# A transformer block on one core: row statistics and normalisation moved ahead of the second tile's maximum in VectorE's order, and the first transposes of the probabilities waiting tile by tile

## The chip, the cores and the metric

The kernel runs on one core of a Trainium2 chip. The metric is the device time of one execution in microseconds, as the median over runs. TensorE (PE), VectorE (DVE), ScalarE (ACT) and GpSimd (POOL) each run their own list of instructions in order and wait for each other by semaphores; SyncE's queue (SP) issues nearly all transfers of the attention loop.

## The reference

One cross-attention block with a feed-forward part, in float32. x is 2 x 2048 x 512, the context 2 x 77 x 512, and there are 16 heads of 32.

```python
xq = layer_norm(x, qn_w, qn_b)
ctx = layer_norm(context, cn_w, cn_b)
q = (xq @ q_w).reshape(B, N, H, D)
kv = (ctx @ kv_w).reshape(B, M, 2, H, D)
attn = jnp.einsum('bnhd,bmhd->bhnm', q, k) * scale
attn = jnp.where(xa_mask[:, None, :, :], neg, attn)
attn = jax.nn.softmax(attn, axis=-1)
out = jnp.einsum('bhnm,bmhd->bnhd', attn, v).reshape(B, N, C)
x = x + out @ proj_w + proj_b
h = layer_norm(x, n2_w, n2_b)
h = gelu(h @ fc1_w + fc1_b) @ fc2_w + fc2_b
return x + h
```

## The kernel before

Every matrix product is made from three passes: each operand is split into a high part (rounded by ScalarE, names that end in h) and a low part (the rest, by VectorE, names that end in l).

The kernel has two stages. The first, the attention pipeline, works on 16 units of 256 rows (two tiles of 128). The second, the feed-forward part, works on 8 blocks of 512 rows and is not touched.

One step k of the pipeline works on four units at once. Of unit k it does the back part: transposes of the probabilities (`prob_T`, out of S), their split into PT (`prob_hi` on ScalarE, `prob_lo` on VectorE), the product with the values (`av`), the projection (`proj`) and the residual, which VectorE adds into xr. Of unit k+1 it does the scores (`score`, four head groups of each of two tiles), the masked copy into S (`masked`), the row maximum (`maximum`, on VectorE), the exponentials (`exps` for tile 0 and `exp_all` for tile 1 on ScalarE) and their normalisation by GpSimd. Of unit k+2 it does the transposes of the normalised rows (`x_T`), their split (`x_hi`, `x_lo`) and the query product (`q`). Of unit k+3 it does the layer norm: `stats` and `variance` on VectorE, `rstd` (a power) on GpSimd, and `normed`, which writes xhat, on VectorE.

Each engine's order is written out by hand in the function `step` of its program. Steps 0 to 9 run in a hardware loop of two steps a round; steps 10 to 15 are written out. Steps 10 to 13 also make one tile of the second layer norm for the feed-forward part (`norm2`: `h_stats`, `h_variance`, `h_normed`, `h_T`, `h_lo`), and steps 10 to 12 are the last with a layer norm of unit k+3. Two preparing steps (`prep`) come ahead.

The places that matter here:

- TensorE begins a step with a score group of tile 0, `x_T(0)`, a score group, `x_T(1)`, then `prob_T1(0, 0)` (three transposes), a score group, `prob_T1(0, 1)`, the last score group of tile 0, and `q(0)`. GpSimd's multiplication of S by 1/sum, one for each tile (L531), counts `p_prob`, and the first transpose waits for both.
- The transposes of the probabilities alternate between two PSUM banks: `v_probT.wait(pe, b, i - 2)`. So the two of group 3, `prob_T(3)`, wait until `prob_lo(2)` has read the banks of group 2, tile by tile. Likewise a score group waits for the masked copy two groups back.
- VectorE's `prob_lo(2)` (L858) stands behind `maximum(1)` (L835) and `av_lo(0)` (L863).
- GpSimd's step is: add the projection's bias to xr, write the mask as numbers, subtract tile 1's maximum from S (L517), `rstd` (L480), and the two multiplications (L531).
- SP stores unit k's result out of its slot of xr once the residual is done, waits for the store to land, and then loads unit k+4 into the same slot. `stats` of step k+1 works on unit k+4 and waits for this load:

```python
v_res.wait(sp, k, UT - 1)
sp.dma_start(x2_units[k.u]..., xr[...]).then_inc(d_x2st, 16)
if more:
    sp.wait_ge(d_x2st, k.q * 32 + (k.u * 16 + 16))
    load_x(k.plus(4))
...
def stats():
    dve.wait_ge(d_x[n.u], n.q * 16 + 16)      # n = k + 3
```

Of the kernel before, what the change touches and what calls it, by code (L numbers as in the profile page):

```python
# [26 lines left out]
P = 128  # L27
# [39 lines left out]
def build_block(nc, x, ctx, mask, qn_w, qn_b, cn_w, cn_b, n2_w, n2_b, q_w, kv_w, proj_w, proj_b,  # L67
# [10 lines left out]
    UT = 2  # L78
# [62 lines left out]
    veps = at("veps", [P, UT], F32)  # L141
    rstd = at("rstd", [P, UT], F32)
# [90 lines left out]
    p_prob = count("p_prob", UT)  # L233
# [15 lines left out]
    v_bn, v_mv, v_veps = count("v_bn", UT), count("v_mv", UT), count("v_veps", 1)  # L249
    p_rstd = count("p_rstd", 1)  # L250
    v_xhat = count("v_xhat", UT)
# [31 lines left out]
    def static(n):  # L283
        return Unit(n // 2, n % 2)
# [185 lines left out]
    def gpsimd_program(pool):  # L470
        pool.memset(mhalf[:, :], -0.5).then_inc(p_half, 1)
        pool.memset(ident[:, :], 0.0).then_inc(p_ident, 1)
        pool.wait_ge(p_ident, 1)
        pool.affine_select(out=ident[:, :], in_=ident[:, :], compare_op=ALU.not_equal, fill=1.0, base=0,
                           pattern=[[-1, P]], channel_multiplier=1).then_inc(p_ident, 1)
        pool.wait_ge(p_half, 1)

        def power(dst, src, n):

            return pool.tensor_tensor(dst, src, mhalf[0:n, 0:src.shape[1]], ALU.pow)  # L480

        pool.wait_ge(v_cve, 1)
        power(crs[0:M, :], cve[0:M, :], M).then_inc(p_crs, 1)
        for b in range(B):
            pool.memset(f32(vbd[:, b, :, :, :]).rearrange("p a b c -> p (a b c)"), 0.0).then_inc(p_zero, 1)

        def may_negate(n):

            pool.wait_ge(d_mask[n.u], n.q * 16 + 16)
            v_scores.wait(pool, n.plus(-2), UT * KT - 1)  # L490

        def negative(n):

            pool.tensor_scalar(negm[:, n.u, :, :], mask_in[:, n.u, :, :], -FLT_MAX, 1.0, ALU.mult,
                               ALU.mult).then_inc(p_neg.sem, 1)

        def step(k, back=False, scores=False, front=False, norm=False, prep=None,
                 norm2=None, split=()):
            def add_projb(t):
                v = xr[:, bass.ds(k.slot(), 1), t, :]  # L500
                pool.tensor_tensor(v, v, projb[:, :].unsqueeze(1), ALU.add).then_inc(p_projb.sem, 1)

            if front:
                may_negate(k.plus(2))
            if back:
                add_projb(0)
            if front:
                negative(k.plus(2))
            if back:
                add_projb(1)  # L510
            if norm2 is not None:
                h_rstd(static(0), norm2)
            if scores:
                n = k.plus(1)
                v_max.wait(pool, n, 1)
                v = S[:, n.u, 1, :].rearrange("p (h m) -> p h m", h=H)
                pool.tensor_tensor(v, v, nmax[:, n.u, 1, :].unsqueeze(2).to_broadcast([P, H, M]),  # L517
                                   ALU.add).then_inc(p_less.sem, 1)
            if norm2 is not None:
                h_bias(static(0), norm2)  # L520
            if norm:
                n = k.plus(3)
                v_veps.wait(pool, n, 0)
                v_xhat.wait(pool, n.plus(-1), UT - 1)
                power(rstd[:, :], veps[:, :], P).then_inc(p_rstd.sem, 1)
            if scores:
                n = k.plus(1)
                for t in range(UT):
                    v_rsum.wait(pool, n, t)
                    v = S[:, n.u, t, :].rearrange("p (h m) -> p h m", h=H)  # L530
                    pool.tensor_tensor(v, v, rsum[:, n.u, t, :].unsqueeze(2).to_broadcast([P, H, M]),  # L531
                                       ALU.mult).then_inc(p_prob.sem, 1)
            if prep == "scores":
                pool.wait_ge(d_projb, 16)

        def h_rstd(n, t):
            v_hve.wait(pool, n, t)
            power(hrs[:, :], hve[:, :], P).then_inc(p_hrs.sem, 1)

        def h_bias(n, t):  # L540

            if isinstance(n.q, int) and n.q == 0 and n.u == 0 and t == 0:
                pool.wait_ge(d_fc2b, 16)
            v_hhat.wait(pool, n, t)
            v = x2[n.u][:, t, :]
            pool.tensor_tensor(v, v, fc2b[:, :], ALU.add).then_inc(p_fc2b.sem, 1)

        pipeline(pool, step)


        def step2(s, first=False, last=False):
            for j in range(JT):
                if not last and j in NORMS:
                    h_rstd(s.plus(1), NORMS.index(j))
                    h_bias(s.plus(1), NORMS.index(j))

        blocks(pool, step2)
# [193 lines left out]
    def vector_program(dve):  # L751
# [10 lines left out]
        for b in range(B):  # L762
            i = dve.bn_stats(cbn[0:M, b, :], cx[0:M, b, :])
        i.then_inc(s_chain, 1)
        dve.wait_ge(s_chain, 1)
        for b in range(B):
            i = dve.bn_aggr(cmv[0:M, b, :], cbn[0:M, b, :])
# [4 lines left out]
        for b in range(B):  # L772
            i = dve.tensor_scalar(cx[0:M, b, :], cx[0:M, b, :], cmv[0:M, b, 0:1], crs[0:M, b:b + 1],  # L773
                                  ALU.subtract, ALU.mult)
# [43 lines left out]
        def step(k, back=False, scores=False, front=False, norm=False, prep=None,  # L818
                 norm2=None, split=()):
            b, s, f, n = k, k.plus(1), k.plus(2), k.plus(3)  # L820

            def masked(t, g_):
                i = t * KT + g_
                if i == 0:
                    p_neg.wait(dve, s, 0)
                    t_probT.wait(dve, s.plus(-2), KT * UT - 1)
                t_scores.wait(dve, s, i)
                dve.tensor_tensor(S[:, s.u, t, g_ * GM:(g_ + 1) * GM].rearrange("p (h m) -> p h m", h=HG),  # L828
                                  s_bank(i, prep)[:, 0:GM].rearrange("p (h m) -> p h m", h=HG),
                                  negm[:, s.u, t, :].unsqueeze(1).to_broadcast([P, HG, M]),  # L830
                                  ALU.add).then_inc(v_scores.sem, 1)
# [20 lines left out]
            def prob_lo(g_, tiles=range(UT)):  # L852
                for t in tiles:
                    i = g_ * UT + t
                    v = slice(t * P, (t + 1) * P)
                    a_probT.wait(dve, b, i)
                    slots, n = new_slots(g_)
                    dve.tensor_tensor(PT[LO][:, slots, v], bT[i % 2][:, 0:n * P].rearrange("p (c n) -> p c n", c=n),  # L858
                                      f32(PT[HI][:, slots, v]), ALU.subtract).then_inc(v_probT.sem, 1)
# [18 lines left out]
            def stats():  # L878
                dve.wait_ge(d_x[n.u], n.q * 16 + 16)
                for t in range(UT):  # L880
                    dve.bn_stats(bnst[:, t, :], xr[:, bass.ds(n.slot(), 1), t, :]).then_inc(v_bn.sem, 1)

            def variance():
                for t in range(UT):
                    dve.bn_aggr(mv[:, t, :], bnst[:, t, :]).then_inc(v_mv.sem, 1)
                v_mv.wait(dve, n, UT - 1)
                dve.tensor_scalar(veps[:, :], mv[:, :, 1], EPS, None, ALU.add).then_inc(v_veps.sem, 1)
# [44 lines left out]
                h_variance(static(0), norm2)  # L932
            if back:
                prob_lo(0, (1,))
            if scores:
                masked(1, 0)
                masked(1, 1)
            if back:
                prob_lo(1)
            if scores:  # L940
                masked(1, 2)
                masked(1, 3)
            if prep == "scores":
                maximum(0)
                x_lo(0)
                x_lo(1)
# [19 lines left out]
                prob_lo(3)  # L966
            if norm2 is not None:
                h_normed(static(0), norm2)
            if norm and prep is None:
                stats()  # L970
                v_bn.wait(dve, n, UT - 1)
            if back:
                av_lo(2)
            if split:
                w1_lo(split[1])
            if norm and prep is None:
                variance()
            if front:
                q_lo(1)
            if back:  # L980
                av_lo(3)
            if scores and prep is None:
                recip(0)
            if norm and prep != "q":
                normed()
            if prep == "scores":
                values_lo(1)
            if scores and prep is None:
                exp_sum()
# [84 lines left out]
    def tensor_program(pe):  # L1074
# [40 lines left out]
        def step(k, back=False, scores=False, front=False, norm=False, prep=None,  # L1115
# [33 lines left out]

            def prob_T1(g_, t):  # L1150
                i = g_ * UT + t
                if i == 0:
                    p_prob.wait(pe, b, UT - 1)
                v_probT.wait(pe, b, i - 2)
                for n, c in enumerate(NEW[g_ % 2]):
                    r = g_ // 2 * 2 * GM + START[c]
                    mm = pe.transpose(bT[i % 2][:, n * P:(n + 1) * P], S[:, b.u, t, r:r + P], ident[:, :])  # L1157
                mm.then_inc(t_probT.sem, 1)
# [194 lines left out]
```

## Time and profile before

| | |
|---|---|
| median of 3 runs | 1138.02 us (1137.82 to 1138.62) |
| span of the profiled execution | 1135.9 us |
| TensorE busy | 1100.3 us (97%) |
| VectorE busy | 606.5 us (53%) |
| ScalarE busy | 404.4 us (36%) |
| GpSimd busy | 234.7 us (21%) |
| mean granted TensorE clock | 0.997 |

The profile is of one execution, whose own time is its span of 1135.9 us; around it lie some 2 us that the runs' times hold besides. Busy shares are means over the two stages. VectorE's busy share by fortieths of the span is 7 to 9 tenths over the attention pipeline (the first 15 slices) and 2 to 4 tenths behind it.

### The profile page before, as it was taken

Reading aid. Unit: us, or ns where it says so; the run is one execution under the profiler, and the core shown is the slowest. Engines: PE = TensorE matmul, PEld = TensorE weight load, DVE = VectorE, ACT = ScalarE, POOL = GpSimd, SP = SyncE. Lnnn points to the kernel's source line nnn. Section 1 sums busy time; section 2 is a strip of 40 time slices with the busy share of each in tenths; the row PEclk is TensorE's granted clock in tenths of the full one; section 3 lists DMA queues with packets and bytes.
Section 4 is the critical chain, followed back from the end, with each engine's and each line's share of the span. In section 5 each row is a group of like instructions: output and inputs, shape, how many; then the busy total and the mean of one; then the engine's idle time right before and its main releaser. Section 6 shows DMA issues by size and latency. Waiting matters only on the chain.

```text
span 1135.9 us, 16366 instructions
## 1 busy us (share of the span) xinstructions
PE 1100.3 (97%) x5849; PEld 941.0 (83%) x5849; DVE 606.5 (53%) x1154; ACT 404.4 (36%) x1158; POOL 234.7 (21%) x186
## 2 busy tenths in 40 slices
PE   4999999999999999999999999999999999999998
PEld 4789988999889888888888888888888888888887
DVE  7898999899999765632423322323333333232212
ACT  3456655566666744421211311221221131121110
POOL 2343444444554420100100100100110110010000
PEclk9999999999999999999999999999999999999999
DMA  7011111232111024202002002002001001100101
GB/s 245 8 35 58 38 38 47 65 93 65 39 57 39 29 91 145 71 19 74 1 1 75 1 2 74 1 1 74 1 1 64 13 1 38 38 1 1 38 1 38
DMA packets 40144, 48.76 MB, mean 43 GB/s; under 512 B 10965, under 2 KB 19197, under 8 KB 40087
## 3 DMA queue, kind: packets, MB, share of 16 engines
q1 hardware_dynamic: 37919, 43.74, 11.7%
q10 hardware_dynamic: 2168, 4.21, 1.0%
q8 instruction: 42, 0.69, 0.2%
q14 instruction: 15, 0.12, 0.0%
HBM read 30.54 MB, written 16.78 MB: 42 GB/s over the span
## 4 chain that ended last, share of the span: by engine, by line
PE 85%; DVE 5%; POOL 4%; issue 3%; ACT 2%; DMA 0%; ACTq 0%; POOLq 0%; DVEq 0%
PE bank L1304 31%; PE bank L1275 31%; PE bank L1144 7%; PE bank L1175 6%; POOL S L531 4%; PE bank L1125 4%; PE bank L1157 3%; ACT S L637 1%; PE bank L1186 1%; PE bank L1287 1%; DVE xhat L893 1%; DVE cx L773 1%; DVE esum L868 0%; PE bank L1135 0%; DVE S L828 0%
## 5 line engine op out<-in xcount | busy, mean ns | idle before, releaser
L1304 PE MATMUL bank<-w,gTh 128*128 128x512 f32 x1024 | 319.3, 393 | 0.0
L1045 DVE CAST gTh<-g 128x512 fp32r<-128x512 f32 x128 | 56.9, 444 | 442.9 <-ACT g L739 442.9
L739 ACT ACTIVATE g<-bank,cols 128x512 f32<-128x512 f32 x128 | 88.0, 688 | 471.6 <-PE bank L1275 470.1
L1304 PEld LDWEIGHTS bank<-w,gTh 128*128 128x128 f32 x1024 | 192.4, 188 | 42.7
L1304 PE MATMUL bank<-w,gTl 128*128 128x512 f32 x512 | 200.4, 391 | 0.0
L1275 PE MATMUL bank<-hT0h,w 128*128 128x512 f32 x512 | 162.2, 397 | 0.0
L1275 PE MATMUL bank<-hT1h,w 128*128 128x512 f32 x512 | 159.1, 392 | 0.1
L480 POOL TENSOR_TENSOR hrs<-hve,mhalf 128x1 f32<-128x1 f32 x32 | 17.6, 549 | 551.3 <-DVE hve L1019 551.3
L1304 PEld LDWEIGHTS bank<-w,gTl 128*128 128x128 f32 x512 | 96.1, 188 | 22.0
L1275 PEld LDWEIGHTS bank<-hT0h,w 128*128 128x128 f32 x512 | 94.7, 188 | 21.5
L1275 PEld LDWEIGHTS bank<-hT1h,w 128*128 128x128 f32 x512 | 95.1, 188 | 19.8 <-issue 0.5
L637 ACT ACTIVATE S<-S,nmax 128x77 f32<-128x77 f32 x256 | 88.9, 354 | 41.8 <-DVE nmax L835 41.8
L1275 PE MATMUL bank<-hT0l,w 128*128 128x512 f32 x256 | 101.1, 395 | 0.0
L1275 PE MATMUL bank<-hT1l,w 128*128 128x512 f32 x256 | 99.7, 389 | 0.0
L1053 DVE TENSOR_TENSOR gTl<-g,gTh 128x512 fp32r<-128x512 f32 x128 | 88.6, 693 | 4.5
L531 POOL TENSOR_TENSOR S<-S,rsum 128x1232 f32<-128x1232 f32 x32 | 75.1, 2346 | 46.1 <-DVE rsum L876 46.1
L1144 PE MATMUL bank<-xTh,wqh 128*128 128x256 f32 x256 | 74.7, 292 | 0.1
L1175 PE MATMUL bank<-PTh,vbd 128*128 128x256 f32 x384 | 73.3, 287 | 0.6 <-DVE PTl L858 0.6
L1144 PE MATMUL bank<-xTl,wqh 128*128 128x256 f32 x256 | 72.8, 285 | 0.0
L1144 PE MATMUL bank<-xTh,wql 128*128 128x256 f32 x256 | 72.8, 284 | 0.0
L723 ACT ACTIVATE bank<-bank,cols 128x128 f32<-128x128 f32 x128 | 47.2, 428 | 66.8 <-PE bank L1287 66.8
L858 DVE TENSOR_TENSOR PTl<-bank,PTh 128x256 fp32r<-128x256 f32 (+1 forms) x128 | 57.6, 482 | 12.0 <-ACT PTh L622 12.0
(103 smaller groups left out, 1824.8 us busy)
## 6 DMA issues: line engine op xcount, KB each, us to landing
xr<-in_x SPq DMA_DIRECT2D x16, 512.0 KB, 3.5
x_scratch<-xr SPq DMA_DIRECT2D x16, 512.0 KB, 2.8
x<-x_scratch SPq DMA_DIRECT2D x8, 1024.0 KB, 5.6
out<-x SPq DMA_DIRECT2D x7, 1024.0 KB, 4.3
w1raw<-in_L_xattn_fc_w SPq DMA_DIRECT2D x16, 256.0 KB, 3.0
w2raw<-in_L_xattn_fc_w SPq DMA_DIRECT2D x16, 256.0 KB, 2.6
kvw<-in_L_xattn_kv_w ACTq DMA_DIRECT2D x2, 1024.0 KB, 11.1
qraw<-in_L_xattn_q_w ACTq DMA_DIRECT2D x1, 1024.0 KB, 11.6
```

The costliest lines, as they stand in the source:

```text
L531: pool.tensor_tensor(v, v, rsum[:, n.u, t, :].unsqueeze(2).to_broadcast([P, H, M]), ALU.mult).then_inc(p_prob.sem, 1)
L637: i = act.activation(v, v, ACT.Exp, bias=nmax[:, s.u, t, h:h + 1], accum_out=esum[:, s.u, t, h:h + 1])
L723: i = act.activation(v, v, ACT.Identity, bias=cols[:, N2B + k:N2B + k + 1], scale=cols[:, N2W + k:N2W + k + 1])
L739: act.activation(g[:, :], bF[j % 2][:, :], ACT.Gelu, bias=cols[:, F1B + j:F1B + j + 1]).then_inc(a_gelu.sem, 1)
L858: dve.tensor_tensor(PT[LO][:, slots, v], bT[i % 2][:, 0:n * P].rearrange("p (c n) -> p c n", c=n), f32(PT[HI][:, slots, v]), ALU.subtract) ...
L1045: dve.tensor_copy(gT[HI][j % 4][:, :], g[:, :]).then_inc(v_ghi.sem, 1)
L1053: dve.tensor_tensor(gT[LO][j % 4][:, :], g[:, :], f32(gT[HI][j % 4][:, :]), ALU.subtract).then_inc(v_glo.sem, 1)
L1125: mm = pe.matmul(s_bank(i, prep)[:, 0:GM], qT[d][:, g_, t * P:(t + 1) * P], kbd[w][:, s.u, g_, :], start=(n == 0), stop=(n == 2))
L1144: mm = pe.matmul(bA[m // 2][:, (m % 2) * UN:(m % 2 + 1) * UN], wq[w][:, c, m * P:(m + 1) * P], xT[d][:, c, :], start=(n == 0), stop=(n == ...
L1175: mm = pe.matmul(bV[g_ % 2][:, 0:UN], vbd[:, b.u, w, g_ * NC + c, :], PT[d][:, slot(g_, i), :], start=(n == 0), stop=(n == 3 * NC - 1))
L1275: mm = pe.matmul(bF[j % 2][:, :], w1[:, j, w, c, :], hT[s.u][d][:, c, :], start=(c == 0 and i == 0), stop=(c == KT - 1 and i == 2))
L1304: mm = pe.matmul(bC[t][:, :], gT[d][j % 4][:, t * P:(t + 1) * P], w2[:, j, w, :], start=(j == 0 and i == 0), stop=(j == JT - 1 and i == 2))
```

## The change

In VectorE's order of the steps with a layer norm (all but the preparing ones), `stats` moves from behind the split of group 3 of the probabilities to ahead of the masked copies of tile 1, `variance` to behind the first two of these, and `normed` to ahead of `maximum(1)`. It used to stand behind the reciprocal of tile 0's sums, ahead of tile 1's sums. GpSimd's `rstd` moves ahead of the subtraction that waits for `maximum(1)`. On TensorE the transposes of group 0 wait for the probabilities of their own tile alone.

```diff
 GpSimd
             if norm2 is not None:
                 h_rstd(static(0), norm2)
+            if norm and prep is None:
+                x_rstd()
             if scores:
                 n = k.plus(1)
                 v_max.wait(pool, n, 1)
...
-            if norm:
-                n = k.plus(3)
-                v_veps.wait(pool, n, 0)
-                v_xhat.wait(pool, n.plus(-1), UT - 1)
-                power(rstd[:, :], veps[:, :], P).then_inc(p_rstd.sem, 1)
+            if norm and prep is not None:
+                x_rstd()
 VectorE
             if back:
                 prob_lo(0, (1,))
+            if norm and prep is None:
+                stats()
             if scores:
                 masked(1, 0)
+            if norm and prep is None:
+                v_bn.wait(dve, n, UT - 1)
+            if scores:
                 masked(1, 1)
+            if norm and prep is None:
+                variance()
             if back:
                 prob_lo(1)
             if scores:
                 masked(1, 2)
                 masked(1, 3)
+            if norm and prep is None:
+                normed()
...
             if norm2 is not None:
                 h_normed(static(0), norm2)
-            if norm and prep is None:
-                stats()
-                v_bn.wait(dve, n, UT - 1)
             if back:
                 av_lo(2)
             if split:
                 w1_lo(split[1])
-            if norm and prep is None:
-                variance()
...
-            if norm and prep != "q":
+            if prep == "scores":
                 normed()
-            if prep == "scores":
                 values_lo(1)
 TensorE
             def prob_T1(g_, t):
                 i = g_ * UT + t
-                if i == 0:
-                    p_prob.wait(pe, b, UT - 1)
+                if g_ == 0:
+                    p_prob.wait(pe, b, t)
                 v_probT.wait(pe, b, i - 2)
```

VectorE, the middle of a loop step, from the second split of group 0 (`prob_lo(0, (1,))`) to the split of group 2. `S` is the masked copy, `nmax` the maximum, `PTl` the low part of the transposed probabilities, `aTl` that of the product with the values. Before:

```order
L858 TENSOR_TENSOR PTl<-bank,PTh 128x3x128 [waits a_probT]
...
L828 TENSOR_TENSOR S<-bank,negm 128x308 [waits t_scores] x2
...
L858 TENSOR_TENSOR PTl<-bank,PTh 128x2x128 [waits a_probT]
...
L828 TENSOR_TENSOR S<-bank,negm 128x308 [waits t_scores]
...
L835 TENSOR_REDUCE nmax<-S 128x16 [waits v_scores]
L64 ISA
L863 TENSOR_TENSOR aTl<-bank,aTh 128x256 [waits a_av]
```

The same place of VectorE now (the lines have moved by 5). `bnst`, `mv` and `veps` are the row statistics, `xhat` the normalised rows:

```order
L863 TENSOR_TENSOR PTl<-bank,PTh 128x3x128 [waits a_probT]
L884 ISA
L886 ISA [waits d_x1]
L886 BN_STATS bnst<-xr 128x6
...
L833 TENSOR_TENSOR S<-bank,negm 128x308 [waits t_scores,v_bn]
L890 BN_AGGR mv<-bnst 128x2 x2
L892 TENSOR_SCALAR veps<-mv 128x2 [waits v_mv]
...
L898 TENSOR_SCALAR xhat<-xr,mv,rstd 128x512 [waits t_xT,p_rstd]
L898 TENSOR_SCALAR xhat<-xr,mv,rstd 128x512 [waits t_xT]
L64 REGISTER_ALU
L840 TENSOR_REDUCE nmax<-S 128x16 [waits v_scores]
```

Seven instructions and the wait for the load of x (`d_x1`, in the other step of a round `d_x0`) now stand between the split of group 0 and that of group 2, which comes right behind the rows shown.

GpSimd, the middle of a loop step, before (`nmax` is the subtraction of the maximum, `rstd` the power):

```order
L501 TENSOR_TENSOR xr<-xr,projb 128x512
L64 ISA
L517 TENSOR_TENSOR S<-S,nmax 128x1232 [waits v_max]
L64 ISA
L64 ISA [waits v_veps]
L480 TENSOR_TENSOR rstd<-veps,mhalf 128x2 [waits v_xhat]
```

and now:

```order
L501 TENSOR_TENSOR xr<-xr,projb 128x512
L64 ISA
L64 ISA [waits v_veps]
L480 TENSOR_TENSOR rstd<-veps,mhalf 128x2 [waits v_xhat]
L64 ISA
L525 TENSOR_TENSOR S<-S,nmax 128x1232 [waits v_max]
```

The power no longer stands behind the wait for the maximum.

## Rows read from the trace of the kernel before

**Rows 1.** Page, busy time of each engine and share of the span
```profile
PE 1100.3 (97%) x5849; PEld 941.0 (83%) x5849; DVE 606.5 (53%) x1154; ACT 404.4 (36%) x1158; POOL 234.7 (21%) x186
```

**Rows 2.** Timeline of TensorE, around a step's start: start, duration, [idle before <-releaser]
```profile
208.95 0.60 PE L1157 MATMUL bank<-ident,S 128*128 128x128 f32 x4
209.31 0.48 PE L1175 MATMUL bank<-PTh,vbd 128*128 128x256 f32 x2
...
218.23 0.39 PE L1186 MATMUL bank<-wph,aTl 128*128 128x512 f32 x1
...
219.73 0.60 PE L1135 MATMUL bank<-ident,xhat 128*128 128x128 f32 x4
221.43 0.55 PE L1157 MATMUL bank<-ident,S 128*128 128x128 f32 x3 [1.09 <-POOL S L531]
...
227.07 0.39 PE L1125 MATMUL bank<-kbdh,qTh 128*128 128x308 f32 x1
...
291.34 0.55 PE L1157 MATMUL bank<-ident,S 128*128 128x128 f32 x3 [1.08 <-POOL S L531]
```

**Rows 3.** Timeline of GpSimd, the two multiplications of S of that step
```profile
214.62 2.51 POOL L531 TENSOR_TENSOR S<-S,rsum 128x1232 f32<-128x1232 f32 x1 [0.99 <-DVE rsum L876]
219.12 2.25 POOL L531 TENSOR_TENSOR S<-S,rsum 128x1232 f32<-128x1232 f32 x1 [2.00 <-DVE rsum L876]
```

**Rows 4.** Timeline of VectorE, layer norm at the end of the step
```profile
210.57 1.27 DVE L881 BATCH_NORM_STATS2 bnst<-xr 128x6 f32 x2
...
212.31 0.24 DVE L885 BATCH_NORM_AGGREGATE mv<-bnst 128x2 f32<-128x6 f32 x2
212.58 0.17 DVE L887 TENSOR_SCALAR veps<-mv 128x2 f32<-128x2 f32 x1
...
214.47 2.94 DVE L893 TENSOR_SCALAR xhat<-xr,mv,rstd 128x512 f32 x2
```

**Rows 5.** Timeline of VectorE, preparing step: the same pair with GpSimd idle
```profile
31.73 1.00 DVE L893 TENSOR_SCALAR xhat<-xr,mv,rstd 128x512 f32<-128x512 f32 x2
```

**Rows 6.** Timeline of VectorE, residual and first half of the next step
```profile
219.16 1.29 DVE L901 TENSOR_TENSOR xr<-bank,xr 128x512 f32 x2
...
221.13 1.28 DVE L841 TENSOR_TENSOR xTl<-bank,xTh 128x512 fp32r<-128x512 f32 x2
...
223.60 0.55 DVE L858 TENSOR_TENSOR PTl<-bank,PTh 128x384 fp32r<-128x384 f32 x1
...
225.40 0.55 DVE L858 TENSOR_TENSOR PTl<-bank,PTh 128x384 fp32r<-128x384 f32 x1
225.87 0.85 DVE L828 TENSOR_TENSOR S<-bank,negm 128x308 f32<-128x308 f32 x2
227.55 0.76 DVE L858 TENSOR_TENSOR PTl<-bank,PTh 128x256 fp32r<-128x256 f32 x2 [0.83 <-ACT PTh L622]
...
229.11 1.44 DVE L835 TENSOR_REDUCE nmax<-S 128x16 f32<-128x1232 f32 x1
...
230.80 1.01 DVE L858 TENSOR_TENSOR PTl<-bank,PTh 128x384 fp32r<-128x384 f32 x2
```

**Rows 7.** Timeline of ScalarE, the high part of `x_T(1)`
```profile
220.37 0.60 ACT L603 ACTIVATE xTh<-bank 128x512 fp32r<-128x512 f32 x1 [0.27 <-PE bank L1135]
```

**Rows 8.** Timeline of SP's queue, the store of x2 and the load of x
```profile
220.75 0.39 SPq L408 DMA_DIRECT2D x_scratch<-xr  x1
223.89 0.38 SPq L369 DMA_DIRECT2D xr<-in_x  x1
```

**Rows 9.** Instructions of line L369, the load of x: issue to landing
```profile
DMA to landing us min/median/max: 3.1/3.5/9.5
```

**Rows 10.** Timeline of TensorE, starts of steps 11 and 12
```profile
313.44 0.63 PE L1135 MATMUL bank<-ident,xhat 128*128 128x128 f32 x4 [0.74 <-DVE hT0l L1030]
...
337.12 0.63 PE L1135 MATMUL bank<-ident,xhat 128*128 128x128 f32 x4 [0.74 <-DVE hT0l L1030]
```

More of the change, by code:

```diff
@@ L510, in step, with x_rstd @@
                 add_projb(1)
+            def x_rstd():
+                n = k.plus(3)
+                v_veps.wait(pool, n, 0)
+                v_xhat.wait(pool, n.plus(-1), UT - 1)
+                power(rstd[:, :], veps[:, :], P).then_inc(p_rstd.sem, 1)
             if norm2 is not None:
                 h_rstd(static(0), norm2)
+            if norm and prep is None:
+                x_rstd()
             if scores:
```

## The prediction

> **What bounds the kernel now.** I read the page first: TensorE is busy for 1100 of 1136 us [rows 1], so only what makes it wait, or takes a wait away, can move the time. The change touches the 16 steps of the attention pipeline alone, about the first 400 us. Next the timeline of TensorE, for what stands in front of its waits. A loop step holds one: after `x_T(1)` it waits for the first transpose of the probabilities, and the profile puts the wait on GpSimd's multiplication of S [rows 2]. The transposes of `x_T(1)` start at 219.73; with no wait the next group follows 0.36 us behind (the step 208.95 to 209.31, also four transposes), at 220.08, but it starts at 221.43: 1.35 us lost. From 221.43 to 291.34 are three steps [rows 2], so a step takes 23.30 us.
>
> Then I ask why the multiplication is late. GpSimd had nothing to do for 2.00 us before tile 1's [rows 3]: it waited for VectorE's sums, which stand behind `normed`. And `normed`, two instructions, took 2.94 us [rows 4], while the same pair takes 1.00 us where GpSimd is idle [rows 5]: in the loop it coincides with the multiplication of tile 0 [rows 3], and its second instruction gets through only when that is done.
>
> **The change, part by part.** I count in us behind the start of `x_T(1)` on TensorE (219.73 in the rows; "at 5.0" is 224.73). The sum is made against the profiled execution (span 1135.9, and 2.1 us more in the median of the runs, 1138.0).
>
> Removed. The tile 1 sums no longer wait for `normed`, so they come up to 2.9 us earlier and the wait of 1.35 us at `prob_T1(0, 0)` goes; I give it back whole. The wait by tiles then costs and brings nothing more: both multiplications are done when TensorE arrives. Without any wait a step would be 21.95 us, and TensorE would reach the score group of tile 1 that stood at 227.07 at 5.99, and `prob_T(3)` at 11.17 (the step's 23.30, less 10.78 from 208.95 to 219.73, less 1.35) [rows 2].
>
> Moved. `stats`, `variance` and `normed` now stand ahead of `prob_lo(2)`, for which `prob_T(3)` waits. So the question is when VectorE has done `prob_lo(2)`. I follow it through the step:
>
> - ScalarE's high part of `x_T(1)` ends at 1.24 [rows 7]; the low part takes 0.64 (half of 1.28), to 1.9; two masked copies 0.8 (0.85 less their overlap with the next), to 2.7; the first split of group 0, the maximum of tile 0 and the second split 0.46 + 1.36 + 0.46 (from 225.40 to 225.87, and 229.11 to 230.80 less the 0.33 of the split between), to 5.0 [rows 6].
> - Now `stats`. It reads x of unit k+3, whose load SP issues only after the residual of the step before is stored. The residual ended at 220.45, and the load was issued at 223.89, 3.44 us later [rows 6, 8]; it lands 3.1 to 3.5 us after that [rows 9], so at 7.3 to 7.7 by the old timing. The old `stats` began at 210.57, some 14 us into the step, and never saw this [rows 4]. In the new order the second residual is no longer held by VectorE but by the projection, whose last matmul ends at 218.62 [rows 2]; with 0.05 for the semaphore and 0.65 for the instruction (half of 1.29) [rows 6] it ends at -0.4, and x lands at 6.1 to 6.5. I take 6.2, a little below the middle, as a choice. VectorE waits 1.2 us, and everything behind it on its queue with it: the masked copies that free the score banks, the splits, the maximum.
> - From 6.2: `stats` 1.2, two masked copies 0.8, aggregate and add 0.44 (212.31 to 212.75) [rows 4], to 8.65. The power on GpSimd is short and hidden behind what follows: two splits and two copies, 1.56 (227.55 to 229.11) [rows 6], to 10.2.
> - `normed`: no multiplication runs on GpSimd here, it has only the maximum's subtraction ahead, which waits for VectorE itself. The bounds are 1.0 [rows 5] and 2.94 [rows 4]; I take 1.0, by what GpSimd does beside it, less 0.08 of overlap, to 11.15.
> - Maximum and split of `av`, 1.69 (229.11 to 230.80), then `prob_lo(2)`, 1.01 for both tiles [rows 6]: done at 13.4 and 13.85.
>
> TensorE, which could be at `prob_T(3)` at 11.2, so waits there until 13.9 for its second half. (It waits earlier too, at 5.99 for the masked copy that is done at 7.9, but that is inside the same sum: from there it reaches `prob_T(3)` at 13.1.) Behind the second half: 0.18 for it, 0.05 for restarting, and 10.42 from the product with the values to the next `x_T(1)` (209.31 to 219.73) [rows 2]. New step: 13.9 + 0.23 + 10.42 = 24.55 us, against 23.30. I round to 1.2 us more a step.
>
> The Trainium skill, "GPSIMD Engine Reference", Key points, says that GpSimd shares its SBUF interfaces with VectorE's instructions in a two-port mode or with two SBUF inputs. By that rule `normed` would be freed of GpSimd in its new place, and the two rows agree (2.94 against 1.00). The Trainium skill, "DMA: Bandwidth & Descriptors", Rules for kernel authors, asks to issue a transfer early and to wait for it late; the change waits earlier for the same issue. By that page's cost of about 2.0 us plus the bytes at 436 GB/s, an estimate of 3.2 us for each of the two 512 KB transfers would set x at 6.3.
>
> **The sum.** Steps 1 to 9: nine times 1.2, 10.8 us. Step 0 has its x from the start, and also had no wait to lose: the moved work is 2.55 us (1.2 + 0.44 + 0.9) on VectorE, less the 0.83 that it idled behind the copies [rows 6] and the 0.8 by which `prob_lo(2)` was early for TensorE (230.80 + 1.0 against 208.95 + 23.3, for the second tile a little less): 0.9 us. Steps 10 to 12 last 23.68 us [rows 10]; they hold 0.9 us more of statistics ahead on VectorE (one half of `stats`, an aggregate and an add), which fill most of the wait for x, and 0.36 for one more group of transposes behind: 24.55 - 1.2 + 0.9 + 0.05 + 0.36, less rounding, 24.3, so 0.6 more each, 1.9. Step 13 begins without the 0.74 that TensorE waited for the low part of hT [rows 10]: -0.7. Together 12.9, rounded down to 12.5: a span of 1148.4 and a time of **1150.5 us**.
>
> **The rivals.**
>
> - *Break-even.* x is there in time, or VectorE's stretch is a little shorter. Then `prob_lo(2)` is done 1.2 us earlier, at 12.65, and TensorE's new wait of 1.5 is about what the old one was: a step of 23.3, and only step 0 and the last ones change, 1138.0 + 2.1 = 1140 us. For it: the old wait does go. Against it: SP's order has not been changed, and 6.1 is the earliest landing that the rows give. Chance, within 0.2% of before (2.3 us, about what runs of this kernel can tell apart): 0.11.
> - *Faster.* The old wait of 1.35 goes and no new one comes: thirteen steps, the last three at 0.7, give 15 us, 1123. It decides at 11.2: VectorE must have done tile 0 of `prob_lo(2)` by then, and needs 2.2 us less than I count, more than the wait for x. Half of it is the price of `normed`, if the pair even overlapped with other work, half x. Chance 0.09.
> - *GpSimd in the way after all.* `normed` still takes 2.94, since what slows it is not the multiplication. Then 1.9 us more in all thirteen steps: 1175 us. Against it: the row of the preparing step. Chance 0.08.
> - *Forecast*: the wait for x and the moved work reach TensorE. Chance 0.72, and its own range is 1143 to 1158: half a us a step either way for the landing (0.4 wide) and the sum of eleven durations.
>
> The range: 1140 to 1159. Below it lie the faster cases, above it the slow `normed`. Slower by over 0.2%: 0.80; within: 0.11; faster: 0.09.
>
> **What would show it.** In the changed profile TensorE should have no wait on GpSimd's multiplication, but waits of 1.5 to 2 us on VectorE's S and of some 0.3 to 0.8 us, twice, on PTl in front of `prob_T(3)`. VectorE should wait for the load of x some 1.2 us in nine steps. `normed` should last 1.0 us a pair. The step should be 24.5 us. The prediction is wrong if the load of x lands before `stats` is reached, if `normed` stays slow, or if VectorE's idle time at the step's end does not let the residual run at once behind the projection: in that case x lands later and the step is longer still.

## The result, and the profile after

The changed kernel takes 1156.54 us in the median of 4 runs (1155.73 to 1157.66), the kernel before 1137.92 on the same chip (4 runs, 1137.57 to 1138.62): a ratio of 1.0162, 95% interval 1.0148 to 1.0177. It is slower, and inside the range of the prediction, 6.0 us above its value.

The page of the changed kernel, the span and the busy times:

```profile
span 1154.3 us, 16392 instructions
...
PE 1110.7 (96%) x5849; PEld 946.8 (82%) x5849; DVE 581.6 (50%) x1154; ACT 406.7 (35%) x1158; POOL 231.9 (20%) x186
```

VectorE is busy for 25 us less than in [rows 1], nearly all of it the 1.95 us by which each of 13 pairs of `normed` got shorter, and yet the profiled execution lasts 18.4 us longer. Its busy total says nothing of when its work is done.

The table of waits of the same kernel (engine, tile and line that waited, its releaser: us in total, times, longest):

```profile
DVE bnst L886 <- DMA xr<-in_x: 15.4, 11, 1.9
...
PEld bank L1165 <- DVE PTl L863: 3.8, 13, 0.6
...
PE bank L1133 <- DVE S L833: 21.6, 13, 2.2
```

TensorE's wait for GpSimd's multiplication [rows 2] is gone. In its place VectorE waits for the load of x (`stats`), and TensorE for VectorE's masked copies of S (line 1133, the score group of tile 1): 0.20 us in step 0, 1.6 to 2.2 us in each of the nine steps behind it and 1.1 to 1.7 us in the last three. It also waits a little for the low parts ahead of `prob_T(3)` (line 1165).

One step, on the timeline of VectorE in the changed kernel:

```profile
205.59 0.69 DVE L906 TENSOR_TENSOR xr<-bank,xr 128x512 f32 x1 [0.98 <-PE bank L1194]
...
211.02 0.55 DVE L863 TENSOR_TENSOR PTl<-bank,PTh 128x384 fp32r<-128x384 f32 x1
213.00 1.28 DVE L886 BATCH_NORM_STATS2 bnst<-xr 128x6 f32 x2 [1.44 <-DMA xr<-in_x]
214.20 0.85 DVE L833 TENSOR_TENSOR S<-bank,negm 128x308 f32<-128x308 f32 x2
...
216.78 0.99 DVE L898 TENSOR_SCALAR xhat<-xr,mv,rstd 128x512 f32 x2
217.69 1.43 DVE L840 TENSOR_REDUCE nmax<-S 128x16 f32<-128x1232 f32 x1
...
219.37 1.01 DVE L863 TENSOR_TENSOR PTl<-bank,PTh 128x384 fp32r<-128x384 f32 x2
```

SP's queue in that step, the store of x2 and the load of x, which answers to [rows 8]:

```profile
206.50 0.39 SPq L408 DMA_DIRECT2D x_scratch<-xr  x1
209.53 0.38 SPq L369 DMA_DIRECT2D xr<-in_x  x1
```

And TensorE's timeline, around the same step and at the start of the next:

```profile
206.56 0.60 PE L1143 MATMUL bank<-ident,xhat 128*128 128x128 f32 x4
207.00 0.49 PE L1165 MATMUL bank<-ident,S 128*128 128x128 f32 x3
...
212.38 0.60 PE L1165 MATMUL bank<-ident,S 128*128 128x128 f32 x4
214.72 0.41 PE L1133 MATMUL bank<-kbdh,qTh 128*128 128x308 f32 x1 [1.74 <-DVE S L833]
...
219.97 0.90 PE L1165 MATMUL bank<-ident,S 128*128 128x128 f32 x4
...
231.06 0.60 PE L1143 MATMUL bank<-ident,xhat 128*128 128x128 f32 x4
```

The transposes of the probabilities now follow `x_T(1)` after 0.44 us (206.56 to 207.00) instead of 1.70 [rows 2]: the old wait has gone. x lands 6.44 us behind `x_T(1)` (213.00), `normed` lasts 0.99 us, `prob_lo(2)` is done at 220.38, 13.8 us behind, and the step is 24.50 us. The chain is the one the prediction drew, and its ends are near the predicted 13.85 and 24.55.

What it did not have is in other steps. The starts of `x_T(0)` on TensorE, from step 1 on:

```
changed kernel                79.79 104.58 129.13 155.13 179.65 205.71 230.19 254.92 281.07 305.42 330.24 354.80 379.05
lasts                              24.79  24.55  26.00  24.52  26.06  24.48  24.73  26.15  24.35  24.82  24.56  24.25
```

Of the nine steps from 79.79 to 305.42 six last 24.57 in the mean, and three last 26.0 to 26.15. The granted clock tells them apart; the windows of the first long one (us, busy time of PE, PEld, DVE, ACT and POOL, granted clock, DMA share, GB/s):

```profile
134.00:138.00 4.00, 2.41 (x20) 2.18 (x19) 2.25 (x5) 3.25 (x16) 0.00 (x0) 1.00 0.49 136
138.00:142.00 4.00, 3.54 (x18) 3.54 (x19) 3.97 (x13) 0.65 (x2) 0.70 (x1) 0.66 0.00 0
142.00:146.00 4.00, 4.00 (x33) 4.00 (x32) 3.04 (x7) 2.96 (x14) 2.25 (x1) 0.91 0.00 0
```

TensorE idles for 1.6 of 4 us while VectorE waits for x, and then its granted clock falls for some microseconds to the lower level, 1.2 GHz (0.66 and 0.91 are means over windows that hold both levels). The matmuls in it take longer, and the step 1.5 us more. The other two long steps have the same at 188 to 196 and at 264 to 272 us. The mean granted clock is 0.992, before 0.997. The Trainium skill, "TensorE: Matmul & The Clock Gate", Part 1, says that an idle TensorE falls back to 1.2 GHz, and of the rise it says that its moment differs from run to run. The trace shows the fall (1.6 us idle, then 0.66), but behind gaps of 2.1 to 2.2 us, shorter than the idle stretch that the page speaks of; here the measurement decides. Of the rise the traces say nothing to this; the falls do differ from run to run (a second profile of this kernel, below).

### The profile page after: what moved, and what is told of

It is laid out like the page before. It is cut to its first block, busy times and chain, and to the rows that moved or that the text cites. A ratio compares the mean times of both kernels' runs of the same rounds, so it can differ in the third digit from the quotient of the medians.

```text
span 1154.3 us, 16392 instructions
## 1 busy us (share of the span) xinstructions
PE 1110.7 (96%) x5849; PEld 946.8 (82%) x5849; DVE 581.6 (50%) x1154; ACT 406.7 (35%) x1158; POOL 231.9 (20%) x186
## 4 chain that ended last, share of the span: by engine, by line
PE 84%; DVE 6%; DMA 6%; issue 1%; ACT 1%; DVEq 0%; SPq 0%; POOL 0%; ACTq 0%; POOLq 0%
PE bank L1312 31%; PE bank L1283 31%; PE bank L1194 8%; PE bank L1183 6%; PE bank L1152 4%; DMA xr<-in_x 3%; DMA x_scratch<-xr 3%; PE bank L1133 2%; PE bank L1165 2%; PE bank L1295 1%; DVE bnst L886 1%; DVE S L833 1%; DVE xr L906 1%; ACT S L642 1%; DVE cx L778 1%
## 5 line engine op out<-in xcount | busy, mean ns | idle before, releaser
L536 POOL TENSOR_TENSOR S<-S,rsum 128x1232 f32<-128x1232 f32 x32 | 72.1, 2253 | 66.5 <-DVE rsum L881 66.5
L1133 PE MATMUL bank<-kbdh,qTh 128*128 128x308 f32 x128 | 45.0, 352 | 21.6 <-DVE S L833 21.6
```

The costliest lines, as they stand in the source:

```text
L1133: mm = pe.matmul(s_bank(i, prep)[:, 0:GM], qT[d][:, g_, t * P:(t + 1) * P], kbd[w][:, s.u, g_, :], start=(n == 0), stop=(n == 2))
```

## The experiments

The kernel before took 1137.76 (14 runs), 1138.04 (7) and 1137.80 us (7) in the three groups of runs (e1 to e4, e5 to e8, e9 to e11), on three chips. "A step" is the mean of those of the nine steps that hold no clock fall; that of the kernel before is 23.32 (209.84 us for nine; the three of [rows 2] give 23.30).

| kernel | us | ratio (95%) | step | clock falls in the profile |
|---|---|---|---|---|
| changed | 1156.54 | 1.0162 (1.0148 to 1.0177) | 24.57 | 3 |
| e1_stats_resident | 1136.07 | 0.9986 (0.9976 to 0.9995) | 22.94 | 0 |
| e2_tile_only | 1132.83 | 0.9958 (0.9944 to 0.9972) | 22.79 | 0 |
| e3_normed_before_recip | 1123.54 | 0.9876 (0.9859 to 0.9892) | 22.15 | 0 |
| e4_after_fill | 1152.81 | 1.0133 (1.0116 to 1.0150) | 24.58 (the first 25.65) | 0 |
| e5_resident_slow | 1164.88 | 1.0236 (1.0219 to 1.0253) | 24.60 | 6 |
| e6_normed_late | 1149.33 | 1.0102 (1.0085 to 1.0119) | 24.19 | 1 |
| e7_order_only | 1154.67 | 1.0143 (1.0126 to 1.0160) | 24.56 | 3 |
| e8_normed_recip_both_tiles | 1123.64 | 0.9873 (0.9857 to 0.9890) | 22.14 | 0 |
| e9_after_again | 1154.14 | 1.0146 (1.0129 to 1.0163) | 24.57 | 2 |
| e10_order_again | 1155.53 | 1.0153 (1.0136 to 1.0170) | 24.54 | 3 |
| e11_after_fill7 | 1153.48 | 1.0138 (1.0121 to 1.0155) | 24.56 (the first 26.07) | 0 |

**Is it the wait for x?** The changed kernel, with the statistics read from rows that have long been in SBUF. Its output is normalised with another unit's statistics; the load and all instructions stay.

```diff
 def stats():
-    dve.wait_ge(d_x[n.u], n.q * 16 + 16)
+    m = f if back else n
+    if not back:
+        dve.wait_ge(d_x[n.u], n.q * 16 + 16)
     for t in range(UT):
-        dve.bn_stats(bnst[:, t, :], xr[:, bass.ds(n.slot(), 1), t, :])...
+        dve.bn_stats(bnst[:, t, :], xr[:, bass.ds(m.slot(), 1), t, :])...
 def normed():
+    if back:
+        dve.wait_ge(d_x[n.u], n.q * 16 + 16)
```

> The changed kernel, but in the loop and the steps behind it the row statistics read the rows of unit k+2, which have been in SBUF for a step, and only the normalisation waits for the load of unit k+3 (so the output is normalised with another unit's statistics; the work is the same). Theory, that the wait for the load of x is what costs: VectorE reaches prob_lo(2) 1.4 to 1.8 us earlier, TensorE's wait on S falls from about 2 us to 0.3 to 0.6 us, a step falls from 24.6 us (undisturbed) to about 23.2, and if the dips of the granted clock in three steps come of the long waits they go too: 1138 to 1142 us. Rival, that the moved vector work alone fills VectorE's stretch and the load only hides in it: no better than 1152 us, with VectorE still waited for about 2 us a step.

1136.07 us, 20.5 less than the changed kernel and below the expected 1138 to 1142. VectorE and TensorE in one of its steps (`x_T(1)` starts at 218.19):

```profile
222.64 0.55 DVE L863 TENSOR_TENSOR PTl<-bank,PTh 128x384 fp32r<-128x384 f32 x1
223.11 1.27 DVE L888 BATCH_NORM_STATS2 bnst<-xr 128x6 f32 x2
...
226.85 1.00 DVE L902 TENSOR_SCALAR xhat<-xr,mv,rstd 128x512 f32 x2
```

```profile
224.02 0.60 PE L1169 MATMUL bank<-ident,S 128*128 128x128 f32 x4
224.82 0.41 PE L1137 MATMUL bank<-kbdh,qTh 128*128 128x308 f32 x1 [0.20 <-DVE S L833]
```

With the same instructions in the same order, `stats` starts at once, TensorE's wait on S shrinks from 1.74 to 0.20 us, the step from 24.57 to 22.94, and no clock fall is left. So the wait for x costs nine times 1.63, 14.7 us, and the falls that come with it 4.5 in the profiled execution; steps 10 to 12 are 0.9 us shorter together. The moved work alone costs no more than the removed wait gave: this kernel is 1.7 us faster than the kernel before.

**The tile-by-tile wait alone**, on the kernel before.

```diff
-                if i == 0:
-                    p_prob.wait(pe, b, UT - 1)
+                if g_ == 0:
+                    p_prob.wait(pe, b, t)
```

> The kernel before with the tile-by-tile wait alone. Theory: the first transpose group goes 1.3 us earlier, the score group behind it too, and only the second group waits for tile 1's multiplication, 0.4 to 0.5 us instead of 1.35: 0.8 to 0.9 us less in each of ten steps, 1129 to 1130 us. Rival, as the prediction's sum had it (the wait by tiles brings nothing by itself, since the order decides): 1137 to 1138 us.

1132.83 us, 5 less than before, 0.53 a step (22.79 against 23.32), where 0.8 to 0.9 a step and 1129 to 1130 us were expected. It agrees with neither side. TensorE and GpSimd:

```profile
217.56 0.49 PE L1157 MATMUL bank<-ident,S 128*128 128x128 f32 x3
218.28 0.41 PE L1125 MATMUL bank<-kbdh,qTh 128*128 128x308 f32 x1 [0.23 <-DVE S L828]
...
218.82 0.55 PE L1157 MATMUL bank<-ident,S 128*128 128x128 f32 x3
```

```profile
216.51 2.25 POOL L531 TENSOR_TENSOR S<-S,rsum 128x1232 f32<-128x1232 f32 x1 [2.00 <-DVE rsum L876]
```

Tile 0's transposes go ahead, but those of tile 1 (218.82) still stand right behind the end of its multiplication (216.51 + 2.25 = 218.76), and the score group between them, which now comes earlier, waits 0.23 for VectorE. So the split hides a part of GpSimd's lateness; 22.79 is still 0.64 above the 22.15 of e3 (below), and that remainder is larger than the expected 0.4 to 0.5. In the old order it is worth something by itself.

**Only `normed` moved, by one place**, on e2: ahead of the reciprocal of tile 0's sums, which starts GpSimd's multiplication.

```diff
+            if norm and prep is None:
+                normed()
             if scores and prep is None:
                 recip(0)
-            if norm and prep != "q":
+            if norm and prep == "scores":
                 normed()
```

> The kernel before with the tile-by-tile wait, and the normalisation moved only past the reciprocal of tile 0, to ahead of it; statistics stay where they were. Theory: the pair of xhat takes 1.0 us instead of 2.94, since GpSimd has not begun to multiply, tile 1's sums come about 2 us earlier, TensorE's wait at the start of a step goes and no other comes: 1.35 us less in ten steps and 0.7 in three, 1120 to 1125 us. Rival (the pair is slow wherever it stands in the loop, or the later reciprocal of tile 0 holds the first transposes): 1134 to 1140 us.

1123.54 us (4 runs, 1123.35 to 1124.15): 1.2% faster than the kernel before, and the best version found. VectorE and GpSimd:

```profile
207.92 0.99 DVE L893 TENSOR_SCALAR xhat<-xr,mv,rstd 128x512 f32 x2
208.82 0.24 DVE L876 RECIPROCAL rsum<-esum 128x16 f32<-128x16 f32 x1
209.22 1.44 DVE L868 TENSOR_REDUCE esum<-S 128x16 f32<-128x1232 f32 x1
210.69 0.25 DVE L876 RECIPROCAL rsum<-esum 128x16 f32<-128x16 f32 x1
```

```profile
209.15 4.46 POOL L531 TENSOR_TENSOR S<-S,rsum 128x1232 f32<-128x1232 f32 x2 [1.71 <-DVE rsum L876]
```

The pair lasts 0.99 us with the multiplication not yet begun, against 2.94 beside it [rows 4], where the multiplication itself took 2.51 us and not 2.25 [rows 3]; the sum over tile 1, a reduction, keeps its 1.44 us beside the multiplication; and the two multiplications run without a gap. The step is 22.15 us, 1.15 less than before, where the prediction gave back 1.35. With TensorE early, the first product of `q` waits a little for the low part of x (its weight load, 3.1 us in 15 times, some 0.2 each), which accounts for the difference.

**The same with the old wait for both tiles** (e3 with `if i == 0: p_prob.wait(pe, b, UT - 1)`).

> The kernel of e3 (normalisation ahead of the reciprocal of tile 0) with the old wait for both tiles. In e3 the second multiplication is done at 213.6, 0.4 us before the first transposes at 214.0. Theory: 1123 to 1124 us, the same as e3, so that the whole gain is the normalisation's place. Rival: the margin is too small and some wait comes back, 1125 to 1130 us.

1123.64 against 1123.54: once both multiplications are in time, the finer wait brings nothing.

**Order without the tile wait**, the changed kernel with the old wait, twice, the second time beside the changed kernel again.

> The changed order with the old wait for both tiles' probabilities. In the changed kernel both multiplications are done 0.6 us before TensorE comes to the first transposes. Theory: 1155.5 to 1157.5 us, the same as the changed kernel. Rival, the wait by tiles carries some of the time: outside this.

> The changed kernel once more, beside the next two on one chip, to compare them within one set of runs: 1155 to 1158 us, with two to four steps in which the granted clock falls.

> The kernel of e7 (the changed order, the old wait for both tiles) beside the changed kernel. In the traces the stretch from the start of step 1 to that of step 13 was 299.7 us in e7 and 299.3 us in the changed kernel, so the 1.9 us between their times would be the start of the program and the number of clock falls. Theory: within 1 us of e9. Rival, that the wait by tiles itself costs in the new order: e9 again some 2 us slower.

1154.67 and 1155.53 us for the old wait, and 1154.14 for the changed kernel itself, against 1156.54 before the experiments. Three of the expected bands are missed, each by less than 1 us: e7 and e9 came out below theirs, and e10 lies 1.4 us from e9, not within 1. The first time the changed kernel was the slower of the two by 1.9 us, the second time the faster by 1.4, so the times don't tell the two apart. The starts of `x_T(0)` say what differs:

```
e9  80.04 104.94 129.51 155.52 180.08 204.72 230.45 255.20 279.66 303.77 328.63 352.90 377.19
         24.90  24.57  26.01  24.56  24.64  25.73  24.75  24.46  24.11  24.86  24.27  24.29
```

The same kernel has two long steps here and had three above, while the others agree within 0.3 us. Steps 1 to 12 together last 299.3 us in the changed kernel, 299.7 in e7 and 299.1 in e10, with three falls each, and 297.2 us in e9 with two. The number of falls is a matter of the run, and with equal falls the wait by tiles makes no difference in the new order.

**Do TensorE's gaps make the clock fall?** The changed kernel with 14 products of 128x128 by 128x256 whose result nobody reads, in the gap ahead of the score group of tile 1; then with 7.

```diff
             if scores and prep is None:
+                if back and norm:
+                    v_res.wait(pe, b.plus(-1), 0)
+                    for _ in range(14):
+                        pe.matmul(bV[0][:, 0:UN], wq[HI][:, 0, 0:P], wq[HI][:, 0, 0:UN], ...)
                 score(1, 2)
```

> The changed kernel with 14 products of 128x128 by 128x256 that nobody reads, put on TensorE in front of score group (1, 2), where it waits 1.7 to 2.1 us for S in the loop (14 take 1.67 us). They add about 1.5 us in step 0 and 0.5 in the last three. Theory, that the granted clock falls in three steps because TensorE stood idle: the clock stays at 1.00 in the whole loop, the 4.4 us that three steps of 26.07 instead of 24.6 us cost go, and the time is 1153 to 1155 us. Rival, that the dips have another cause: they stay, and the time is 1157 to 1160 us.

> e4 with 7 products in place of 14, so that TensorE stands idle about 1 us a step in place of 2. Theory, that it takes the full idle time of the changed kernel for the clock to fall: clock 0.997 and 1151 to 1153 us (less filling in the steps that wait less than 1.7 us than in e4). Rival, that an idle time of 1 us a step already brings some of the falls: clock 0.993 to 0.996, 1153 to 1156 us.

1152.81 and 1153.48 us, each 0.2 to 0.5 us outside its theory's band, e11 with its time in the band of its rival; the profiled clock is 0.997 in both, as the theories said. The windows of e4 that answer to those above:

```profile
134.00:138.00 4.00, 4.00 (x35) 4.00 (x34) 2.41 (x5) 1.91 (x10) 0.09 (x1) 1.00 0.41 136
138.00:142.00 4.00, 3.78 (x30) 3.58 (x30) 3.96 (x12) 1.76 (x8) 0.70 (x1) 1.00 0.00 0
142.00:146.00 4.00, 3.97 (x34) 3.67 (x33) 4.00 (x9) 3.31 (x14) 1.90 (x1) 1.00 0.00 0
```

The load is the same (136 GB/s), VectorE still waits for x, and TensorE has no fall. The slowest run of e4 (1153.74) lies below the fastest of the changed kernel's eight (1153.91): with more work it is 1.3 to 3.7 us faster. The falls are thus of TensorE's idling. With 7 products the runs of e11 (1152.66 to 1154.65) and of the changed kernel overlap, and two of its four show a mean clock of 0.996, as the profiled run of e6 does with its one fall; so a fall in a run that was not profiled can't be excluded. The rest of the loss stays: the steps still take 24.6 us, and the first of the nine is longer in both (25.65 and 26.07 at full clock), behind a longer wait for x (2.6 and 3.0 us).

A long gap does not bring a fall each time. In the changed kernel TensorE waited the same in step 1, where the clock stayed at 1.00, as in step 3, where it fell:

```profile
89.13 0.41 PE L1133 MATMUL bank<-kbdh,qTh 128*128 128x308 f32 x1 [2.06 <-DVE S L833]
...
138.46 0.41 PE L1133 MATMUL bank<-kbdh,qTh 128*128 128x308 f32 x1 [2.05 <-DVE S L833]
```

The kernel before has a gap of 1.1 to 1.2 us in each of ten steps [rows 2] and no fall in them.

**Without any wait for a load**: e1 with one maximum over 128x1536 on VectorE ahead of `stats`, whose result nobody reads.

```diff
+                if back:
+                    v_dum.wait(dve, k.plus(-1), 0)
+                    dve.tensor_reduce(cols[:, 28:31], f32(wq[HI][:, 0:3, :]), AX.X, ALU.max).then_inc(v_dum.sem, 1)
                 for t in range(UT):
```

> The kernel of e1 (statistics of rows that are resident, so no wait for a load) with one maximum over 128x1536 that nobody reads on VectorE ahead of the statistics in each step: about 1.65 us, by 1.36 us for 1232 elements, in place of the 1.4 to 1.8 us that VectorE waits for the load in the changed kernel. Theory, that what the load costs is the delay of VectorE and nothing of the transfer itself, and that the granted clock falls when TensorE stands idle for 2 us: steps of 24.6 us, one or more steps of 26 us with a granted clock of 0.6 to 0.8 in a 4 us stretch, 1152 to 1158 us. Rival, that the clock fell by something that the load brings: no dip, every step 24.6 us, 1151 to 1153 us, clock 0.997.

1164.88 us. VectorE and TensorE, and two windows of a fall:

```profile
212.72 1.74 DVE L890 TENSOR_REDUCE cols<-wqh 128x3 f32<-128x1536 f32 x1
214.38 1.27 DVE L892 BATCH_NORM_STATS2 bnst<-xr 128x6 f32 x2
```

```profile
216.08 0.41 PE L1141 MATMUL bank<-kbdh,qTh 128*128 128x308 f32 x1 [1.87 <-DVE S L834]
```

```profile
164.00:168.00 4.00, 2.35 (x13) 2.35 (x14) 3.97 (x13) 1.67 (x7) 0.70 (x1) 0.82 0.00 0
168.00:172.00 4.00, 4.00 (x28) 4.00 (x28) 4.00 (x8) 2.73 (x11) 1.88 (x1) 0.75 0.00 0
```

1.66 us of work in the place of 1.3 to 1.9 us of waiting gives about the same wait of TensorE (1.87), the same step (24.60) and falls of the same kind, with no DMA at work in these windows (0.00). So what counts is how late VectorE is at this place, not by what. The load of x still runs here, as it does in e1 and e4, which have no fall. The time came out above the expected 1152 to 1158 us: step 0 and the last three steps have no wait for x, or one of at most 0.5 us, whose place the added work could take. TensorE's gap in the last three grows to 2.7 us, each of them holds a fall and lasts 27.1 us, and with the one in step 0 and two in the nine there were six falls.

**Where does TensorE wait?** The changed kernel with `normed` alone put back to just ahead of `recip(0)`, so that 1 us less stands ahead of `prob_lo(2)` and nothing changes ahead of the masked copies.

```diff
                 masked(1, 3)
-            if norm and prep is None:
-                normed()
...
                 av_lo(3)
+            if norm and prep is None:
+                normed()
             if scores and prep is None:
                 recip(0)
```

> The changed kernel with the normalisation taken out of the stretch ahead of the maximum and put ahead of the reciprocal of tile 0, at the step's end: VectorE has 0.9 us less to do ahead of prob_lo(2). The prediction's sum ends with TensorE waiting for prob_lo(2): by that a step falls by 0.9 us, 1144 us or less. Rival, read from the changed kernel's trace: TensorE already waits 2 us for the masked copy of tile 1 that the statistics and the load hold up, and from there it reaches prob_T(3) 0.1 us before prob_lo(2) is done, so only the last 0.3 to 0.4 us of a step go: 1151 to 1154 us, less if the clock dips go with it.

1149.33 us, steps of 24.2. TensorE in one of them:

```profile
161.62 0.41 PE L1133 MATMUL bank<-kbdh,qTh 128*128 128x308 f32 x1 [1.72 <-DVE S L833]
...
166.81 0.60 PE L1165 MATMUL bank<-ident,S 128*128 128x128 f32 x4
```

The wait on S is as in the changed kernel, and the wait at `prob_T(3)` is gone: 0.60 us for the group, not 0.90. Of 1 us less work only 0.4 us a step comes back, since the larger part of TensorE's loss lies ahead, at the score group. The profiled execution (1146.5 us) is 7.8 us shorter than that of the changed kernel: 3.4 are these nine steps, 3 the two falls fewer, and 1.1 the last three steps. The time lies below the rival's 1151 to 1154 us, which left the falls open, and far above the 1144 us of the prediction's sum.

## Why the prediction was right, and where it was off

- **The old wait goes**: right. Its worth in a step is 1.15 us and not 1.35 (e3), because TensorE next meets the low part of x, which the prediction did not look for.
- **x lands at 6.2, VectorE waits 1.2**: the mechanism was right (e1), the size too low. x lands 6.4 to 6.7 us behind `x_T(1)` (213.00 and 237.77 against 206.56 and 231.06), VectorE waits 1.3 to 1.9 in the nine steps, and a step pays 1.63 for it (e1). The issue comes 3.03 us after the store (206.50 to 209.53) and the landing 3.47 after the issue; the second residual ended at -0.3, where the prediction had -0.4. The prediction's estimate of 3.2 us for each transfer uses a cost that the Trainium skill, "DMA: Bandwidth & Descriptors", Anatomy of one DMA, gives for transfers issued by GpSimd, while SP issues these two; 3.03 and 3.47 are what they took here.
- **`normed` in 1.0**: right (0.99), and e3 shows the cause, the multiplication on GpSimd. The rival "GpSimd in the way after all" falls.
- **`prob_lo(2)` done at 13.85, a step of 24.55**: measured 13.8, and 24.57 in the mean of six steps. That it fits so closely is partly luck. x came 0.24 us later than the 6.2 chosen, and from there to the end of `prob_lo(2)` VectorE took 7.38 us (213.00 to 220.38), where the sum has 7.65. So a step without the wait for x lasts 22.94 us (e1) and not the 23.3 of the break-even rival.
- **Where TensorE waits**: half right. The prediction named both places and took the end of the step from `prob_T(3)`. TensorE loses some 2.0 us at the score group of tile 1 (2.34 us from 212.38 to 214.72, 0.36 without a wait) and some 0.3 to 0.4 at `prob_T(3)` (e6), where two waits of 0.3 to 0.8 were forecast. The sum came out right since one chain of VectorE's work sets both.
- **The tile-wise wait brings nothing**: right in the new order (e7, e9, e10 and e8), and no statement about the old one, where it alone saves 5 us (e2).
- **The sum**: step 0 +0.8 (79.79 against 78.96; 0.9 predicted); nine steps of 24.57 instead of 23.32, 11.3 (10.8 predicted); steps 10 to 12 +1.7 (73.63 against 71.97 us; 1.9 predicted); the rest of the span +0.1 (-0.7 predicted). Together 13.9 against the 12.9 that was rounded to 12.5.
- **Steps 10 to 13**: the working has three slips. The terms printed for a new step add up to 24.66 and not to 24.3; measured are 24.82, 24.56 and 24.25. The step before was taken as 23.68 for all three, but the first of them lasted 24.64 (288.80 to 313.44 between the starts of `x_T(0)`). And the three steps already hold the three waits of 0.74, so the 0.7 taken off for step 13 is counted twice. Put right, the working gives 2.0 us for these steps together, where the prediction has 1.2 and 1.8 were measured.
- **What was missing**: the clock. Three falls at 1.5 us, together 4.5 us and no term of the sum, bring it to 18.4, the measured difference of the spans (1154.3 less 1135.9). The prediction took TensorE's wait as time lost and not as a cause of slower work behind it. That is three quarters of the 6 us by which it was low.

Not tried: a kernel that gets x earlier, say by a slot of its own for the load, which then need not wait for the store of x2. What the new order is worth with a timely x is known only from e1 (1136.07 us, with another unit's statistics), and that is still 12.5 us slower than e3.

## What to carry to other kernels

When work is taken out from in front of a late instruction, ask where it goes: each operand it needs has a time of landing, and an in-order engine that waits for it early makes everything behind it late. Here 1.15 us a step were to be had by moving one pair of instructions over one reciprocal, and the move of the whole block to a place where its load has not landed lost 1.25 us a step instead. A wait of TensorE can have a second price, the clock, which belongs into the sum as a term with a chance of its own: here about 1.5 us for each fall, of which the same kernel had three in one run and two in another.

## What the runs showed of the hardware

- With gaps of 1.1 to 2.2 us, one in each of twelve steps of some 24.6 us, the granted clock fell in 3 of them (changed kernel), at 1.5 us each, in 2 (e9) and in 1 (e6). With 1.86 us in ten steps and 2.7 us in three it fell in 3 of the ten and in all three (e5), at 1.2 us each among the nine. No profile shows a fall in the kernel before (1.1 to 1.2 us in ten steps), in e1 (0.2 us, and 1.1 in three steps), in e2 (0.2) or e3 (none), nor in e11, where the 7 products left gaps of 0.2 to 1.2 us and one of 2.5.
- Unread matmuls in a gap can make a kernel faster: 1152.81 with 14 of them a step, against 1154.14 and 1156.54 without; with 7 it is not clear from the times (1153.48).
- Two float32 `tensor_scalar` of 128x512 take 2.94 us beside GpSimd's multiplication of two SBUF tiles and 0.99 without (e3), and that multiplication takes 2.51 instead of 2.25; a reduction of 128x1232 takes 1.44 in both cases.
